# Pauses between the row gathers of a mixture-of-experts tail, and fewer gathers ahead of the first stores

## The reference, cut to what matters

```
h = tok(x)                                       # (32, 938, 128)
h = h + recurrence(layernorm(h))
h = h + experts(layernorm(h))

def experts(x):                                  # E, F, CAP = 8, 512, 1024
    probs = softmax(x_flat @ Wr, axis=0)         # over the rows
    vals, idx = top_k(probs.T, CAP)              # 1024 rows per expert
    selected = x_flat[idx]
    hid = gelu(einsum('ecd,edf->ecf', selected, W1) + b1)
    out_e = einsum('ecf,efd->ecd', hid, W2) + b2
    return zeros.at[idx].add(vals[..., None] * out_e)
```

## Time and profile before

| | |
|---|---|
| median of 3 timed runs | 578.6 us (576.7 to 583.95) |
| span of the profiled execution, first to last instruction | 605.3 us |
| issue of the last store in it | 595.93 to 597.49 us, so 7.8 us of the span lie behind it |
| POOL busy | 298.7 us (49%) |
| DVE busy | 425.8 us (70%) |
| PE busy | 397.3 us (66%) |

### The profile page before, as it was taken

How to read it: one execution, slowest core, us unless ns; L and a number is a source line. 1 busy time by engine, 2 the same in 40 slices (tenths; PEclk the granted TensorE clock), 3 DMA queues, 4 the chain that set the end, 5 groups by cost and what they waited for, 6 DMA issues and landing times.

```text
span 605.3 us, 11347 instructions
## 1 busy us (share of the span) xinstructions
PE 397.3 (66%) x3577; PEld 320.0 (53%) x3577; DVE 425.8 (70%) x1653; ACT 292.2 (48%) x560; POOL 298.7 (49%) x213
## 2 busy tenths in 40 slices
PE   5798898999888889997000033210199989997900
PEld 5786788865877788764000022110057667775700
DVE  3877878898488887898888878911787658866100
ACT  2787840076699740177545500120258667686400
POOL 0467830058478730076000007776235687888774
PEclk9999999999899999999555555555579989999965
DMA  8679606699888227699999501121011344443332
GB/s 162 132 183 272 150 15 162 142 253 241 194 148 148 58 48 157 201 275 254 323 318 318 190 0 44 49 52 48 17 28 61 67 74 67 65 75 44 31 30 22
DMA packets 86116, 77.44 MB, mean 128 GB/s; under 512 B 15022, under 2 KB 82930, under 8 KB 85810
## 3 DMA queue, kind: packets, MB, share of 16 engines
q1 hardware_dynamic: 68674, 64.52, 41.6%
q0 software_dynamic: 10368, 8.40, 9.8%
q10 hardware_dynamic: 7024, 3.89, 2.7%
HBM read 52.27 MB, written 39.39 MB: 151 GB/s over the span
## 4 chain that ended last, share of the span: by engine, by line
PE 32%; DVE 21%; issue 14%; DMA 10%; POOL 10%; ACT 6%; another core or an unknown queue 5%; SPq 1%; ACTq 1%; DVEq 0%; POOLq 0%
PE banks L1003 7%; POOL out L1843 7%; PE banks L1030 5%; PE banks L929 5%; PE banks L1133 4%; PE banks L1146 4%; PE banks L1040 3%; DMA xin<-in_x 3%; ACT xn L680 2%; PE banks L915 2%; DMA ring<-toeplitz 2%; DVE xn L1512 2%; DMA const<-constants 1%; DVE xn L1576 1%
## 5 line engine op out<-in xcount | busy, mean ns | idle before, releaser
L1829 POOL DMA_INDIRECT hid<-kept,index x64 | 65.0, 1015 | 115.6 <-DVE index L1624 97.0
L1214 DVE BATCH_NORM_STATS2 stats<-hid 120x6 f32<-120x128 f32 (+1 forms) x512 | 104.9, 278 | 19.8 <-ACT hid L671 19.4
L1843 POOL DMA_INDIRECT out<-hid,index x56 | 88.6, 1582 | 25.9 <-issue 16.3
L929 PE MATMUL banks<-const,xt 128*120 128x128 f32 x512 | 74.0, 290 | 12.0 <-ACT xt L666 11.5
L775 ACT ACTIVATE xt<-banks 128x480 f32<-128x480 f32 x64 | 36.3, 570 | 84.9 <-PE banks L1030 83.7
L929 PEld LDWEIGHTS banks<-const,xt 128*120 128x120 f32 x512 | 63.9, 192 | 20.7 <-ACT xt L666 14.4
L1751 POOL TENSOR_TENSOR small<-small,powers 120x16 f32<-120x16 f32 (+2 forms) x18 | 47.9, 2662 | 47.1 <-DVE small L1232 47.1
L1819 POOL TENSOR_TENSOR small<-small,powers 120x16 f32<-120x16 f32 x15 | 43.2, 2901 | 41.7 <-DVE small L1232 36.3
L1003 PE MATMUL banks<-xn,ring 122*120 122x128 f32 x512 | 58.9, 276 | 6.3 <-DMA xn<-s 3.1
L1146 PEld LDWEIGHTS banks<-w_ring,xn 128*128 128x128 f32 x512 | 60.5, 196 | 3.9 <-issue 3.9
L1003 PEld LDWEIGHTS banks<-xn,ring 122*120 122x120 f32 x512 | 57.6, 189 | 7.4 <-issue 6.9
(11 more groups left out here) (222 smaller groups left out, 705.1 us busy)
## 6 DMA issues: line engine op xcount, KB each, us to landing
kept<-out SPq DMA_DIRECT2D x1, 15008.0 KB, 50.5
xin<-in_x SPq DMA_DIRECT2D x28, 480.0 KB, 6.9
out<-hid SPq DMA_DIRECT2D x14, 960.0 KB, 11.1
w_ring<-in_L_ffn_W SPq DMA_DIRECT2D x16, 256.0 KB
ring<-toeplitz SPq DMA_DIRECT2D x32, 112.5 KB
toeplitz<-ring SPq DMA_DIRECT2D x6, 545.0 KB, 11.3
out<-hid SPq DMA_DIRECT2D x2, 784.0 KB
xin<-in_x SPq DMA_DIRECT2D x4, 384.0 KB
```

The lines of the kernel that those rows point to most:

```text
L929: mm = pe.matmul(banks[0:L, 2 + n % 4, i * D:(i + 1) * D], xt[:, n % 2, i, :], cut["basis_t"], start=True, stop=True)
L1214: ins = dve.bn_stats(stats[:, slot, b, :], hid[:, bass.ds(c * HB + b, 1), :].rearrange("p a k -> p (a k)"))
L1829: pool.indirect_dma_start(found[:, n, :], None, kept, bass.IndirectOffsetOnAxis(ap=index[:, n:n + 1], axis=0)).then_inc(found_in[e], 16)
L1843: pool.indirect_dma_start(rows, at_rows, adds[:, n, :], None, compute_op=ALU.add, oob_is_err=True, bounds_check=ROWS * FRAMES - 1).then_in ...
```

## The change

The first burst of gathers is cut from 54 to 40, four gathers instead of two stand behind each expert's stores, and in the burst POOL stops behind gather 16 and behind gather 32. It waits for the rows of the last 8 gathers issued (`found_in[1]`, then `found_in[3]`) and then clears the unused tile `e2` (256 floats in each partition) eight times, each clear waiting for the one before it. Nothing that is computed changes.

```diff
-FOUND_FIRST = 54
+FOUND_FIRST = 40
 WEIGHED_AFTER = {3: (3, 5), 5: (5, 7), 6: (7, 8)}
-FOUND_BETWEEN = 2
+FOUND_BETWEEN = 4
+BURST, PAUSES = 16, 8
...
+        paced = sem("paced")
...
+            def pause(n):
+
+                if n:
+                    pool.wait_ge(paced, n)
+                pool.memset(e2[:, :, :], 0.0).then_inc(paced, 1)
+
             pool.wait_ge(kept_in, 16)
             for n in range(FOUND_FIRST):
+                if n and n % BURST == 0:
+                    pool.wait_ge(found_in[n // SLOT_TILES - 1], 128)
+                    for step in range(PAUSES):
+                        pause(PAUSES * (n // BURST - 1) + step)
                 find(n)
             n = FOUND_FIRST
             for e in range(E):
```

## The result

The changed kernel takes 599.99 us (median of 3 runs, 598.73 to 600.57) against 578.6: slower by 3.5%, ratio 1.0349 with a 95% interval of 1.0271 to 1.0426. The forecast was 600.

The account below looks back on a forecast made before the run. POOL's gathers and adding stores were taken to set the tail's pace. Terms -4.3 + 18.2 + 11.4 - 2.1 - 1.5 = +21.7 (21.5 by the two ends), set on the 578.6 median, gave 600 us; range 586 to 609.

Parts of the forecast that it names:

- The stalls aren't in the timed runs: DVE's three remote waits in `choose(4)` and `choose(5)`, 28 us in the trace, were claimed absent from the timed runs.
- small waits: Waits in POOL's tail, some 1.5 us, that were to go with the change.
- Pauses hidden: In POOL's burst, both pauses, with 4.0 us of clears each, end before DVE delivers expert 0 at 431.4: no cost.
- Cut of the burst: Expert 0's stores start when DVE delivers, at 431.4 instead of 435.7: a gain of 4.3 us.
- fourteen gathers in the tail: Gathers moved between stores on POOL, which sets the pace: 14 x 1.3 = +18.2 us.
- Last gathers too late: Expert 7 completes only at 547.7, so POOL waits for `answer(6, 0)` until 559.4: +11.4 us, the wait less its gap.
- The scan: DVE's scan delays a gather in POOL's burst: 1.9 us on the stores before the change, hidden after it.
- Stalls cured: Rival: DVE's stalls are in the timed runs too and the pauses remove them, -5.8 us, 573; chance 0.14.
- stalls that stay: Rival: DVE's stalls are real and remain, the new tail takes 160.3 us, +22, 601; chance 0.08.
- POOL with slack: Rival: without the profiler POOL issues stores faster, down to PE's 15.1 us per expert, +14 to 15, 593; chance 0.10.

Follow-up runs that it names:

- order_only: Kernel before with 40 gathers first and four between stores, without pauses: 602.91 us, ratio 1.0411.
- fifty_first: Kernel before with 50 gathers first and three between stores, instead of 54 and two: 578.74 us, ratio 1.0015.

## Why the prediction was right

**The stalls aren't in the timed runs.** Right, and the decisive step. I had reconstructed the tail without them; the second trace of the kernel before shows that tail.

| from the first gather, us | worked out | measured |
|---|---|---|
| before: first store | 73.2 | 73.9 |
| before: last store ends | 207.7 | 207.1 |
| changed: first store | 68.9 | 68.0 |
| changed: gather 63 ends | 185.2 | 184.6 |
| changed: last store ends | 229.2 | 228.5 |
| difference of the ends | 21.5 | 21.4 |
| of it: first store | -4.3 | -5.9 |
| of it: first store to last | +25.8 | +27.3 |

That the difference came out within 0.1 us is luck: the first store gained 1.6 us more than forecast and the tail lost 1.5 us more. The term of 1.5 us of small waits that were to go was read from the trace with the stalls (waits of 1.14 and 0.52 us before adding stores, where the usual gap is 0.30); the kernel before profiled again has none but its two landing waits, so there was nothing to go.

The reason that I leaned to was wrong: I gave the stalls to the profiler, with two pages of the Trainium skill beside it ("Runtime: NRT & Kernel Launch", the preamble/postamble breakdown, and "NOTIFIC — the notification-queue block", section 7.1). Every later trace was profiled too, eight of them, three without pauses, and none has a remote wait on DVE in that place. What held was the comparison of the span with the median. The span of each timed run beside the experiments is on record too: the 20 of the kernel before have 573.6 to 581.4 us. Time less span is 1.8 us both in the changed kernel (599.99 and 598.2) and in the kernel before profiled again (576.61 and 574.8), so a span of 605.3 belongs to an execution of some 607 us, and none of the 23 timed runs of the kernel before is above 583.95. By the same 1.8 us the reconstructed span of 578.0 belonged to a time of 579.8 and not to the median itself, which fits as well. No run here shows the 6.2 us that the first page puts between a profile's total and the reported time: a profile's total isn't on record, and its span from the first to the last instruction is shorter than the time.

**Pauses hidden.** Right: order_only and the changed kernel end at the same place. A pause was 4.0 us of clears in the prediction and 2.9 in the trace, inside the bounds; both together were 2.2 us cheaper than worked out, and DVE delivered 0.9 us sooner than worked out (68.0 against 68.9), so POOL's wait ahead of the first store was 4.5 us instead of 3.5. The 0.31 us that a clear takes by itself is what the straight line between the two older sizes gives.

**Cut of the burst and fourteen gathers in the tail.** Right in the sum, but the two terms, -4.3 and +18.2, are one thing. Counted as POOL's idle time it is simpler: the kernel before has none ahead of the first store, the changed one has two pauses and a wait, 4.3 + 4.3 + 4.2 = 12.8 us above the ordinary gaps. That I kept them as two terms is why fifty_first was expected to gain.

**Last gathers too late.** Right in place and size: 12.15 us measured from gather 63 to the next store, 11.7 worked out (547.7 to 559.4). In idle time the changed kernel has it instead of one landing wait: 12.8 + 11.9 - 2.2 = 22.5, less 1.3 us that its gathers and stores took less in all (162.7 against 164.0), makes 21.2 against 21.4.

**The scan.** Right that it recurs, and too high for the kernel before. There the gather beside the scan of `extract(3)` takes 2.37 us, 1.4 above the usual 0.94 and not 1.9, and in the changed kernel 2.82. First the kernel before profiled again, then the changed kernel:

```profile
403.10 2.16 DVE L1576 TENSOR_TENSOR_SCAN xn<-xin,xn 128x960 f16<-128x960 f16 x1
403.64 2.37 POOL L1829 DMA_INDIRECT hid<-kept,index  x1 [0.30 <-issue]
```

```profile
383.06 2.16 DVE L1578 TENSOR_TENSOR_SCAN xn<-xin,xn 128x960 f16<-128x960 f16 x1
...
403.60 2.16 DVE L1578 TENSOR_TENSOR_SCAN xn<-xin,xn 128x960 f16<-128x960 f16 x1
```

A gather that starts while a scan runs ends 0.75 us behind the scan's end, at 406.01 behind 405.26 in the one kernel and at 406.51 behind 405.76 in the other, and what it loses depends on how early in the scan it starts. The forecast named one such gather in the trace that it read. The next scan costs another in both traces of the kernel before: the one profiled again has a gather of 1.85 us from 383.61, with a scan from 382.55 to 384.71. In the changed kernel that scan falls on the landing wait and the first clears of the first pause, and the clears weren't held, for all sixteen take the same time (ns, least, median and most):

```profile
L1856 POOL MEMSET e<- x16: 311/311/312, 384.2 to 413.4; 128x256 f32 x16
```

The scan costs nothing after the change, as forecast, since POOL waits 4.51 us ahead of the first store all the same. The held gathers and the free clears fit the exclusive port pair of the Trainium skill ("SBUF — State Buffer", the text under its diagram of the ports), where a DVE operation with two SBUF inputs holds off only a POOL operation that reads SBUF, if the work for a gather counts as such a read; the runs don't show which port is held.

**The rivals.** Stalls cured (573) and stalls that stay fall with the second trace of before. POOL with slack (593) falls: the traced durations, with their gaps of 0.30 us, give 21.4 us, as the medians do.

## What to carry to other kernels

When one engine issues a fixed list of work back to back, count its idle time from first to last item, since moving items about gains nothing unless it removes idle, and loses when an item lands behind one that needs it. Before a wait in a trace is attacked, set the span against the timed runs: a stall that the median has no room for isn't there to be won. And a pause is free only in slack that exists without it; here the pauses were free because the new order had opened the slack at the price of the tail.

## What was unexpected of the hardware

In one execution DVE took PE's results up to 25 us after their matmuls (5.05, 11.57 and 11.54 us of remote waits, the last two 13.3 us apart in start), and in none of the eight traces taken later. What caused it, and whether the pauses would prevent it, stays open: it didn't come again, with or without pauses.

Clears, too, can be held, though not by a scan. With 24 of them the first pause took 9.44 us and the second 8.79. Three times 2.89, with the two gaps of 0.06 us between the rows of eight, is 8.79, so only the first was dearer. The views are of DVE, then of the clears in the same stretch and in the second pause:

```profile
388.74 2.12 DVE L1564 TENSOR_SCALAR ring<-setup,bounds 128x1024 f16<-128x1024 f16 x4
```

```profile
L1856 POOL MEMSET e<- x8: 311/397/472, 387.9 to 391.2; 128x256 f32 x8
```

```profile
L1856 POOL MEMSET e<- x24: 311/311/313, 418.6 to 427.1; 128x256 f32 x24
```

Four clears beside the four operations of line 1564 took 0.47 us instead of 0.31, which makes the 0.65 us.
